# One 1024-wide scan per state in the chunks that begin a batch, with a reset token between the channel halves

## The reference

```
xn = layernorm(x);  s = mixer(xn);  g = silu(experts0(xn));  x = x + s * g
xn = layernorm(x);  s = attn(xn);   g = silu(experts1(xn));  x = x + s * g
```

```
dt = softplus(dbl[:, :64] @ W_dt + b_dt);  A = -exp(A_log)
dA = exp(dt[..., None] * A);  dBx = (dt * xc)[..., None] * Bm[:, :, None, :]
h = dA_t * h + dBx_t
y = einsum('bdn,bn->bd', h, C_t)
```

## Time and profile before

| what | value |
|---|---|
| time, median of 3 runs | 1128.32 us (1124.17 to 1129.85) |
| span of the profiled execution | 1123.9 us (its own time is not listed apart) |
| DVE busy | 960.6 us, 85% of the span |
| PE busy | 895.5 us, 80% |
| POOL busy | 613.3 us, 55% |
| ACT busy | 607.2 us, 54% |
| mean granted PE clock | 0.916 |

### The profile page before, as it was taken

The page is one execution under the profiler, slowest core; times in us unless marked ns, Lnnn a source line. Parts: engine busy times, 40 slices in busy tenths (PEclk is TensorE's granted clock), DMA queues, the critical chain, the costliest instruction groups (busy, mean ns, idle before and its releaser), DMA issues.

```text
span 1123.9 us, 16984 instructions
## 1 busy us (share of the span) xinstructions
PE 895.5 (80%) x4556; PEld 633.1 (56%) x4556; DVE 960.6 (85%) x1804; ACT 607.2 (54%) x1593; POOL 613.3 (55%) x422
## 2 busy tenths in 40 slices
PE   3466688778787778897997799898876888889878
PEld 1344466556565555675665466665555656556556
DVE  4698878999999998998999899999969878978445
ACT  2444556574456564665666466665554555546243
POOL 1238423768634846675327855665874747425540
PEclk9986789997898898999999899999977999989999
DMA  9955344356543644565444645455742466446201
GB/s 277 298 128 133 85 101 110 119 133 180 118 101 106 141 102 117 148 164 146 111 96 127 156 129 150 102 162 145 192 111 73 109 155 159 109 102 142 73 9 34
DMA packets 168650, 144.71 MB, mean 129 GB/s; under 512 B 15680, under 2 KB 135536, under 8 KB 168560
## 3 DMA queue, kind: packets, MB, share of 16 engines
q10 hardware_dynamic: 39776, 67.47, 27.5%
q1 hardware_dynamic: 121104, 60.43, 18.9%
q0 software_dynamic: 7680, 15.74, 4.6%
HBM read 106.88 MB, written 36.70 MB: 128 GB/s over the span
## 4 chain that ended last, share of the span: by engine, by line
DVE 37%; PE 32%; issue 15%; ACT 8%; DMA 4%; POOL 3%; ACTq 1%; DVEq 0%; SPq 0%; another core or an unknown queue 0%; POOLq 0%
DVE pA L1429 14%; PE pM L996 5%; PE pH L902 5%; DVE hj L1465 4%; PE pM L986 3%; PE p L961 3%; DVE ca L1377 2%; PE pG L958 2%; DVE hj L1477 2%; DVE hc L1437 2%; PE pH L974 2%; DMA bcb<-bc_rows 2%; PE pU L959 2%; POOL dBx L805 1%; PE pG L961 1%
## 5 line engine op out<-in xcount | busy, mean ns | idle before, releaser
L805 POOL TENSOR_TENSOR dBx<-dtx,bcb 128x1024 f32<-128x1024 f32 (+1 forms) x144 | 304.6, 2116 | 364.7 <-DVE pA L1429 339.0
L902 PE MATMUL pH<-const,hc 128*128 128x128 f32 x1024 | 161.8, 305 | 42.3 <-DVE hc L1437 38.8
L1016 ACT ACTIVATE pA<-dt,am 128x512 f32<-128x512 f32 (+1 forms) x288 | 173.9, 639 | 17.2 <-DVE hc L1437 9.5
L1429 DVE TENSOR_TENSOR_SCAN pA<-pA,carry,dBx 128x512 f32<-128x512 f32 (+1 forms) x160 | 162.8, 1063 | 19.5 <-ACT pA L1016 14.4
L902 PEld LDWEIGHTS pH<-const,hc 128*128 128x128 f32 x1024 | 129.0, 157 | 62.9 <-DVE hc L1437 47.1
L1437 DVE TENSOR_TENSOR hc<-pA,bcb 128x1024 f32<-128x1024 f32 (+1 forms) x144 | 159.3, 1106 | 5.0
L1429 DVE TENSOR_TENSOR_SCAN pA<-pA,dBx 128x512 f32<-128x512 f32 x128 | 149.8, 1215 | 13.8 <-ACT pA L1016 8.8
L986 PE MATMUL pM<-const,hj 128*128 128x128 f32 (+3 forms) x636 | 127.7, 297 | 34.2 <-DVE hj L1477 14.2
L747 POOL DMA_INDIRECT rows_in<-xn,slots x120 | 131.6, 1096 | 30.3 <-issue 29.1
L1196 ACT ACTIVATE yj<-pM 128x128 f32<-128x128 f32 x236 | 65.5, 277 | 129.9 <-PE pM L996 119.8
L986 PEld LDWEIGHTS pM<-const,hj 128*128 128x128 f32 (+3 forms) x636 | 71.4, 138 | 107.9 <-issue 75.2
(11 more groups left out here) (208 smaller groups left out, 1530.9 us busy)
## 6 DMA issues: line engine op xcount, KB each, us to landing
bcb<-bc_rows ACTq DMA_DIRECT2D x112, 512.0 KB
rows_out<-yj SPq DMA_DIRECT2D x236, 64.0 KB
xg<-rows_in SPq DMA_DIRECT2D x176, 64.0 KB
bcb<-bc_rows ACTq DMA_DIRECT2D x32, 256.0 KB
rows_in<-gy SPq DMA_DIRECT2D x8, 512.0 KB, 8.9
mixed<-s_st SPq DMA_DIRECT2D x12, 256.0 KB
so<-rows_out SPq DMA_DIRECT2D x6, 512.0 KB
sr<-mixed SPq DMA_DIRECT2D x6, 512.0 KB
```

Of the source, the lines that this page charges most:

```text
L805: pool.tensor_tensor(dBx[:, N % 2, :, 0:t1 - t0], dtx[q % 2][:, :, t0:t1], row, ALU.mult).then_inc(dBx_ready, 1)
L902: last = mm(pH[:, half, c * DI + k * P:c * DI + (k + 1) * P], hc[:, N % 2, k, t * P:(t + 1) * P], ident, is_transpose=True, start=(n == 0 ...
L1016: A(pA[:, k, 0:t1 - t0], dt[q % 2][:, k, t0:t1], ACT.Exp, scale=am[:, k, n:n + 1]).then_inc(decay_ready, 1)
L1429: dve.tensor_tensor_scan(pA[:, k, 0:w], pA[:, k, 0:w], dBx[:, N % 2, k, 0:w], carry[:, k, N % NS:N % NS + 1] if N in carry_after else 0.0, ...
```

## The change

In steps of the chunks 0, 2, 4 and 6 one scan runs over pA as 1024 consecutive elements; it waits for both decays and adds 2 to `h_ready`. So that nothing is carried from the last token of half 0 to the first of half 1, dt of that one token is set to 1e34 after dtx has been computed, which makes its decay 0. `am` (the negative A) is held at -1e-30 or below, so that the product is never 0. `dt_ready` is given after that write in these chunks, and so behind dtx. POOL's wait changes for the product that follows such a step: `h_ready` 2N-2, the scans of step N-2.

```
+RESET = 1e34
...
+def one_scan(N):
+
+    return SEGS[N // NS][0] % 2 == 0
...
                     if N:
-                        pool.wait_ge(h_ready, 2 * N - 1)
+                        pool.wait_ge(h_ready, 2 * N - 2 if one_scan(N - 1) else 2 * N - 1)
...
-                        dve.tensor_scalar(am[:], am[:], -1.0, None, ALU.mult).then_inc(decay_negated, 1)
+                        dve.tensor_scalar(am[:], am[:], -1.0, -1e-30, ALU.mult, ALU.min).then_inc(decay_negated, 1)
...
-                    dve.tensor_tensor(dt[q % 2][:], dt[q % 2][:], xs[:, :, 0:HALF], ALU.add).then_inc(dt_ready, 1)
-                    dve.wait_ge(dt_ready, q + 1)
+                    added = dve.tensor_tensor(dt[q % 2][:], dt[q % 2][:], xs[:, :, 0:HALF], ALU.add)
+                    if q % 2:
+                        added.then_inc(dt_ready, 1)
+                        dve.wait_ge(dt_ready, q + 1)
+                    else:
+                        link(added)
                     dve.wait_ge(xc_ready, DK * (q + 1))
                     dve.tensor_tensor(dtx[q % 2][:], dt[q % 2][:], xc[q % 2][:], ALU.mult).then_inc(dtx_ready, 1)
+                    if q % 2 == 0:
+                        dve.wait_ge(dtx_ready, q + 1)
+                        dve.memset(dt[q % 2][:, 1, 0:1], RESET).then_inc(dt_ready, 1)
...
-                    for k in range(DK):
+                    if one_scan(N):
+                        dve.wait_ge(decay_ready, 2 * N + 2)
+                        both = pA[:].rearrange("p k t -> p (k t)")
+                        dve.tensor_tensor_scan(both, both, dBx[:, N % 2].rearrange("p k t -> p (k t)"), 0.0, ALU.mult, ALU.add
+                                               ).then_inc(h_ready, 2)
+                    for k in range(0 if one_scan(N) else DK):
```

## The result

| | before | changed |
|---|---|---|
| time, median | 1128.61 us (4 runs, 1124.17 to 1129.85) | 1170.05 us (4 runs, 1168.35 to 1172.51) |
| ratio | | 1.0373, 95% interval 1.0335 to 1.0412 |
| span of the profiled execution | 1123.9 us | 1170.7 us (its time 1172.51 us) |
| DVE busy | 960.6 us, 85% | 1001.9 us, 86% |
| mean granted PE clock | 0.916 | 0.881 |

The account below looks back on a forecast made before the run. DVE was taken as the bound in chunk 2 and likely in chunks 0, 4 and 6. Scan gain -4 x 0.8, decay waits +4.5, products +21.3 and write +0.5 gave +23 us: 1151, stated as 1150 us, range 1130 to 1168.

Parts of the forecast that it names:

- the 21.3 us for the products: Chunks 0, 2, 4, 6: DVE stalls beside moved POOL products that reach the end, 10.4 us plus 10.9 us; bounds 0 and 40.
- 30 us of stalls: Chunks 0, 2, 4, 6: added time that DVE's SBUF-only instructions lose beside the moved products, before any share is taken.
- the lower count: Stalls counted only on DVE instructions that start after the product: 38.4 - 8.6 = 30 us more.
- the wide count: Stalls counted from the first SBUF-only DVE instruction in a product to its end: 53.2 - 13.0 = 40 us more.
- 60% in chunks 0, 4 and 6, 90% in chunk 2: Shares of stalls reaching the end: 90% of 11.6 us in chunk 2, 60% of 18.1 us in the other three.
- The decay waits: One scan waits for the second decay in 17 late steps: 9 us, of which 4.5 us taken (0 to 9).
- The scan's gain: One scan of 1024 takes 2.28 us against 2.34 us for the pair: 4 us gained over 64 steps.
- The rest: Element write 0.5 us in all; later dt_ready at the start, am's second operation and larger h_ready count put at nothing.
- A: Rival: faster; stalls fall only into time DVE would have waited anyway, the scans' gain stays: 1122 us, chance 0.08.
- C: Rival: the wait for both decays is the whole cost, no stall at all: +5, 1133 us, chance 0.10.
- B: Rival: nothing to see; half the products stay, 4 us of gain meet 4 to 8 us of loss: 1130, chance 0.10.
- D: Rival: heavy case; running instructions lose too (40 us), gy 5, decay waits 9, passed on at 80%: 1168 us, chance 0.14.

Follow-up runs that it names:

- small products: POOL's product covers only 8 tokens of each half, in the changed kernel and in the kernel before: 1119.74 us and 1113.32 us.
- the first experiment: Kernel before with two scans; only POOL's product wait in chunks 0, 2, 4 and 6 moved to the scans two steps before: 1165.7 us, ratio 1.0303.
- The even delay: Kernel before plus three batch-norm statistics on DVE behind hc in each of 64 steps, 38 us in all: 1148.11 us, ratio 1.0184.
- the placed delay: Kernel before plus 222 batch-norm statistics on DVE in 32 steps where DVE instructions grew with only the product moved: 1160.41 us, ratio 1.0242.
- the kernel with the product beside the scan: Changed kernel, but the product also waits for the gate directly ahead of scan N-1 on DVE: 1134.35 us, ratio 1.0033.

## Why the prediction was wrong

**Right in mechanism and sign, wrong in one term.** The product's new place was forecast as what decides, and it is: moved alone it costs 34 us, and with small products the loss falls from 42 us to 6 us (0 to 13). The start as the latest of scan, load and POOL's queue held in the steps looked at. The term that failed is the 21.3 us for the products. It was made of 30 us of stalls and of the shares of them that reach the end, 0.71 on average. Both were too small: with only the product moved, 37.0 us of stalls and 34 us of time were measured, a share of 0.92.

**The first step that failed: 30 us of stalls.** The excess grew by 37.0 us when only the product moved and by 43.1 us in the changed kernel. Yet the reason for taking the lower count, that a running DVE instruction is mostly not hurt, held on the whole. In the trace of the first experiment 54.6 of the 57.2 us of excess in chunks 0, 2, 4 and 6 lie on DVE instructions that began after a POOL instruction did; before it was 18.0 of 20.4 us. So the growth is theirs, and the count of the lower kind missed 7 us of its own: by chunk it had 6.1, 11.6, 8.8 and 3.2 us, and 9.3, 12.9, 11.3 and 3.3 us were measured. That the wide count came to 40 us, in between 37.0 and 43.1, was luck in this respect.

Two things were missing. One is that a product which yields ends later. These rows of steps 39 and 10 after show it:

```profile
340.14 1.22 DVE L1565 TENSOR_TENSOR gy<-gy,so 128x1024 f32<-128x1024 f32 x1
340.23 3.34 POOL L811 TENSOR_TENSOR dBx<-dtx,bcb 128x1024 f32<-128x1024 f32 x1 [5.92 <-DMA bcb<-bc_rows]
...
122.11 1.23 DVE L1412 SCALAR_TENSOR_TENSOR xs<-xs,ca 128x1024 f32<-128x1024 f32 x1
122.98 2.56 POOL L811 TENSOR_TENSOR dBx<-dtx,bcb 128x1024 f32<-128x1024 f32 x1
123.37 3.25 DVE L1413 SCALAR_TENSOR_TENSOR xs<-v,xs 128x1024 f32<-128x1024 f32 x1
```

L1565 keeps its 1.22 us, the product takes 3.34 us, and what follows reads PSUM and loses nothing. L1412 keeps its 1.23 us too, but L1413 behind it, of the same shape, loses 2.0 us. The count should have moved the product to the end of the running instruction, not cut it short. The other missing part is POOL's gy work, named and then left out: step 35 alone has 6.76 us of excess after and 2.57 us before, and with small products gy's new place makes 3.7 us of excess. How the 7 us divide between the two was not measured.

The Trainium skill (SBUF — State Buffer, "Who interferes with whom") says that of a VectorE and a GpSimd instruction that contend, the one which issues first holds the shared ports for the whole instruction, and the other blocks. By their start times the rows of L1565 and L1412 agree. The L1406 of the earlier trace rows does not, nor does this one of step 10 after, which started 0.26 us ahead of the product and lost 2.47 us:

```profile
118.91 3.16 DVE L1408 TENSOR_SCALAR xs<-ca 128x1024 f32<-128x1024 f32 x1 [1.67 <-ACT ca L1144]
119.17 2.35 POOL L811 TENSOR_TENSOR dBx<-dtx,bcb 128x1024 f32<-128x1024 f32 x1
```

**The second step that failed: 60% in chunks 0, 4 and 6, 90% in chunk 2.** With 70% overall the 37.0 us of the first experiment would be 26 us; 34 us were measured (29 to 40 by the interval). The share was read from the idle time of whole chunks. The stalls do not fall evenly: they fall in steps with much SBUF-only work on DVE, and there, by the trace of the first experiment, they lengthened the steps by 41.9 us for 42.9 us of excess. The even delay passed on 0.7 of the busy time it added, as the prediction has it; the placed one lengthened its steps nearly in full. By the total, though, the placed delay gave 27 us on 38.1 us busy, a share of 0.6 to 0.85 by its interval. So how much of the 34 us is the place stays open. The rest may be chance or PE's clock, which was 0.873 to 0.888 with the moved product and 0.889 to 0.898 with the placed delay; no run tells these apart.

**The decay waits** came out right in sum: 4.5 us taken, 6 us measured (2 to 9). In part that is luck: DVE's waits for decays grew by 15.3 us, not by the 9 us of the count, and 0.4 of them reached the end, not half. **The scan's gain** of 4 us was not there to be measured; the row's 2.29 us is right. **The rest** (write, `am`, start): the kernel with the product beside the scan holds them, the joined scan and the decay waits together, and is 4 us (1 to 7) slower than the kernel before, where the decay waits alone cost 6 us, so they can't be more than a few us. Sum of the parts: 34 + 6 = 40 us, measured 42 us.

**The rivals.** A (faster) and C (only the waits) are refuted; B too. D, 1168 us with 0.14, was the nearest: its stalls, 40 us and 5 us of gy, are close to the 43.1 us measured, and its share of 80% lies nearer to the measured one. Its reason, that running instructions lose too, holds for a small part alone, 6.9 of the 63.7 us of excess in these chunks after.

## What to carry to other kernels

A wait that looks stricter than its buffer needs may be there for what runs beside it: ask what the released instruction will overlap, where two engines are seen to hold each other up on SBUF, before relaxing it. Here the old wait put POOL's 2.36 us beside two DVE instructions with a PSUM operand, and joining those two scans took away the signal that did it. When stalls are counted, read how much reaches the end from the steps in which they fall, not from a chunk's mean idle time.

## What the runs showed of the hardware

- A running DVE instruction can make POOL wait (2.36 us became 3.34 us beside L1565), but the opposite was seen too: DVE's L1406 started 0.11 us ahead of the product and still lost 2.33 us, and xs<-ca (L1408 after), with a lead of 0.25 to 0.39 us, lost 2.47 to 2.61 us in seven of the traces. I did not find what tells the two apart.
- The products cost even the kernel before much: with 8 tokens a product it took 1113.32 us, 1.6% less (1.1 to 2.1%), though POOL is not the bound (55% busy). The excess fell from 26.1 to 4.5 us. How much of that is stalls and how much waiting for products was not separated.
- In no trace of the kernels before and after was a DVE instruction with a PSUM operand more than 0.1 us longer beside POOL's work than the shortest of its form: the scan, hc and the gates kept their times.
- A joined scan of 1024 elements (2.29 us) is no faster in effect than two of 512 back to back (2.34 us), since these overlap at their seam.
